# Perceiver block on one core: ten row buffers for the experts, and the turned input weight kept in memory between the batches

## What is computed

```python
x = x + xattn(layernorm(x), ctx)       # softmax(q k^T) v, q from x, k and v from ctx
x = x + ssm(layernorm(x))              # below
x = x + moe(layernorm(x))              # 8 experts, each token goes to the one with the largest gate

def ssm(x):
    xn = layernorm(x)
    xz = xn @ in_w.T + in_b            # in_w: 1024 x 512, two halves: u and z
    u, z = xz[..., :512], silu(xz[..., 512:])
    y = causal_convolution(u)          # length 512, done with sine and cosine tables
    return clip((y * z) @ out_w.T + out_b + x, -10, 10)

def moe(xt):                           # 1024 tokens
    sel = argmax(softmax(xt @ gate_w + gate_b))
    return (xt @ expert_w[sel] + expert_b[sel])
```

## Time and profile before

| | |
|---|---|
| median of 3 runs | 1106.79 us (1106.1 to 1108.63) |
| the profiled execution | 1108.95 us, its span 1107.1 us |
| PE busy | 1070.4 us (97%), weight loads 870.1 us (79%) |
| DVE, ACT, POOL busy | 854.1 us (77%), 537.4 us (49%), 539.5 us (49%) |
| mean granted clock of PE | 0.987 |
| DMA | 182.26 MB, 165 GB/s over the span |
| chain that ended last | PE 81%, DVE 7%, issue 4%, POOL 3%, DMA 2%, SPq 2%, ACT 1% |

### The profile page before, as it was taken

How to read it: one execution, slowest core, us unless ns; L and a number is a source line. 1 busy time by engine, 2 the same in 40 slices (tenths; PEclk the granted TensorE clock), 3 DMA queues, 4 the chain that set the end, 5 groups by cost and what they waited for, 6 DMA issues and landing times.

```text
span 1107.1 us, 16363 instructions
## 1 busy us (share of the span) xinstructions
PE 1070.4 (97%) x4873; PEld 870.1 (79%) x4873; DVE 854.1 (77%) x1786; ACT 537.4 (49%) x1145; POOL 539.5 (49%) x585
## 2 busy tenths in 40 slices
PE   7999999999999999999999999999999999998697
PEld 6887887788888888887778888888888888886585
DVE  7863688898888888888777777777777657799694
ACT  5222165565555555544664444444444443457371
POOL 2544064445444544411276656665766543227365
PEclk9999999999999999999999999999999999999699
DMA  8221577977767777422358877766776552015992
GB/s 299 86 77 38 94 187 192 215 200 199 186 180 189 193 182 186 152 79 90 81 124 202 195 187 197 194 182 182 184 207 172 174 155 77 1 50 192 344 368 92
DMA packets 199398, 182.26 MB, mean 165 GB/s; under 512 B 17920, under 2 KB 144928, under 8 KB 199346
## 3 DMA queue, kind: packets, MB, share of 16 engines
q1 hardware_dynamic: 178706, 140.21, 48.8%
q10 hardware_dynamic: 17280, 31.46, 8.1%
q0 software_dynamic: 3360, 9.97, 2.5%
HBM read 141.73 MB, written 41.68 MB: 166 GB/s over the span
## 4 chain that ended last, share of the span: by engine, by line
PE 81%; DVE 7%; issue 4%; POOL 3%; DMA 2%; SPq 2%; ACT 1%; POOLq 0%; ACTq 0%; DVEq 0%
PE bank L659 41%; PE bank L823 28%; PE bank L668 3%; PE bank L1101 2%; PE bank L676 1%; PE bank L923 1%; DMA vrows<-in_L_attn_log_dt_dram 1%; POOL hl_F L2178 1%; PE bank L1039 1%; DMA resid<-mixed,gather_rows 1%; DMA resid<-p_rows 1%; DVE probs L392 1%; POOL hl_B L2185 1%; POOL spectra L2348 1%; PE bank L876 0%
## 5 line engine op out<-in xcount | busy, mean ns | idle before, releaser
L1251 ACT ACTIVATE probs<-bank,nbias 128x512 f32<-128x512 f32 x128 | 88.2, 689 | 240.1 <-DVE nbias L1750 240.0
L823 PE MATMUL bank<-hl_F,probsT 128*128 128x512 f32 x768 | 190.1, 396 | 1.9 <-issue 1.6
L823 PE MATMUL bank<-hl_A,probsT 128*128 128x512 f32 x768 | 189.9, 396 | 0.0
L659 PE MATMUL bank<-hl_B,hl_D 128*128 128x512 f32 x768 | 186.4, 392 | 2.4 <-POOL hl_B L2185 2.4
L659 PE MATMUL bank<-hl_C,hl_D 128*128 128x512 f32 x768 | 186.2, 391 | 0.0
L1745 DVE TENSOR_REDUCE mx<-bank 128x1 f32<-128x512 f32 x128 | 87.9, 687 | 119.2 <-PE bank L659 119.2
L823 PEld LDWEIGHTS bank<-hl_F,probsT 128*128 128x128 f32 x768 | 144.0, 188 | 36.4 <-issue 1.9
L659 PEld LDWEIGHTS bank<-hl_B,hl_D 128*128 128x128 f32 x768 | 143.8, 188 | 35.1 <-issue 3.3
L823 PEld LDWEIGHTS bank<-hl_A,probsT 128*128 128x128 f32 x768 | 144.0, 188 | 33.9 <-POOL hl_A L2178 0.3
L659 PEld LDWEIGHTS bank<-hl_C,hl_D 128*128 128x128 f32 x768 | 144.2, 188 | 32.4
L2178 POOL TENSOR_TENSOR hl_F<-stage,hl_F 128x512 fp32r<-128x512 f32 x64 | 85.7, 1339 | 163.6 <-ACT hl_F L1216 163.6
(11 more groups left out here) (468 smaller groups left out, 1852.7 us busy)
## 6 DMA issues: line engine op xcount, KB each, us to landing
p_rows<-probs ACTq DMA_DIRECT2D x120, 256.0 KB, 3.3
stage<-in_ctx_dram SPq DMA_DIRECT2D x112, 256.0 KB, 3.1
spectra<-in_ctx_dram SPq DMA_DIRECT2D x64, 256.0 KB, 5.8
xb<-in_ctx_dram SPq DMA_DIRECT2D x64, 256.0 KB, 5.8
resid<-p_rows SPq DMA_DIRECT2D x240, 64.0 KB, 2.0
h<-p_rows SPq DMA_DIRECT2D x120, 64.0 KB, 2.6
obB<-p_rows SPq DMA_DIRECT2D x120, 64.0 KB, 2.0
stage<-in_L_ffn_expert_w_dram SPq DMA_DIRECT2D x6, 1024.0 KB, 5.8
```

What stands on the lines that cost most here:

```text
L659: last = nc.tensor.matmul(dst, lhs[:, a, t, k * P:(k + 1) * P], rhs[:, c, t, :], start=(t == 0 and (a, c) == PASSES[0]), stop=(t == T - 1 ...
L823: last = nc.tensor.matmul(obank[u % 2][:], probsT[u % 2][:, a, j, :], nat[b][par][:, c, j, :], start=(j == 0 and (a, c) == PASSES[0]), sto ...
L1251: nc.scalar.activation(dst, src, ACT.Exp, bias=nbias[:, q:q + 1], scale=SCALE, accum_out=rsum[:, q:q + 1]).then_inc(probs_ready, 1)
```

## The change

The number of row buffers goes from 8 to 10; the two new ones are `probs` and `h`, four arrays of 2 KB that now lie together as `narrow`. The gathers 8 and 9 are issued with the first eight. The jobs `inT0` and `inT1` of batch 1 are gone. In the middle SP stores `hlB` and `hlC` as they are (high and low) to `in_w_kept`, and at the head of its tail POOL loads them back, once the last scores that read them are done. ACT waits for the stores before it overwrites the two, PE for the loads before `u` and `z`. ACT writes the inverse table before, not after, the second half of batch 0's spectrum. SP loads `out_w` earlier.

```diff
-ROWS_KEPT = 8
+ROWS_KEPT = 10
...
-TAIL_JOBS = (tiles_at(1, "inT0", "pooledT", "inT1") + [f"GT.{n}" for n in range(4)] + tiles_at(1, "x_attn")
+TAIL_JOBS = (tiles_at(1, "pooledT") + [f"GT.{n}" for n in range(4)] + tiles_at(1, "x_attn")
...
-AFTER = [JOB[f"inT0.0@{b}"] for b in range(B)]
+AFTER = [JOB["inT0.0@0"], JOB["pooledT.0@1"]]
...
+        narrow = sb("narrow", [P, 4, CH])
+        probs = [narrow[:, n] for n in range(2)]
...
+        h = [narrow[:, 2 + n] for n in range(2)]
...
-        kept = [spectra[:, 2 * n:2 * n + 2, :] for n in range(4)] + [m[:, 2 * n:2 * n + 2, :] for m in (resid0, qc1) for n in range(2)]
+        kept = [spectra[:, 2 * n:2 * n + 2, :] for n in range(4)] + [m[:, 2 * n:2 * n + 2, :] for m in (resid0, qc1, narrow) for n in range(2)]
```

SP, in `load_natural`, in the middle and behind batch 1's attention:

```diff
+                if b == 1 and c >= NCH:
+                    return
...
                 load(f"chunk{c}@1", ctx_rows[NCH + c])
+                sp.wait_ge(evacuated, EVAC[f"inT{c}.3@0"])
+                sp.dma_start(in_w_kept[c], (hlB, hlC)[c][:].bitcast(F32).rearrange("p a t n -> p (a t n)")).then_inc(in_w_put[c], 16)
...
+            sp.wait_ge(nat_split, B * STEPS - T)
+            load("out_w", matrix(out_w))
             sp.wait_ge(p_moved, B * MOVED)
...
-            sp.wait_ge(filled, JOB["inT0.3@1"] + 1)
-            load("out_w", matrix(out_w))
```

PE, in `attention` and `tail`:

```diff
-                pe.wait_ge(in_nat[b][0], 16 * T * (NCH // 2))
...
-                transposes(f"inT0.#@{b}", stage[0])
+                if b == 0:
+                    pe.wait_ge(in_nat[b][0], 16 * T * (NCH // 2))
+                    transposes(f"inT0.#@{b}", stage[0])
                 weigh(TRIPS - 1, UN - 1)
...
+                pe.wait_ge(in_w_back[0], 16)
                 for k in range(T):
                     evacuated_from(f"normT.{k}@1")
                     product(open_bank(f"u.{k}@1")[:], hlA, k, hlB).then_inc(filled, 1)
+                pe.wait_ge(in_w_back[1], 16)
                 z_tiles(range(1))
```

ACT, in `first_chunk`, `attention` and `tail`:

```diff
+                    act.wait_ge(in_w_put[0], 16)
...
+                if b == 1:
+                    act.wait_ge(in_w_put[1], 16)
...
-                round_scaled("inT0.#@1", hlB)
                 round_rows("pooledT.#@1", hlA)
+                act.wait_ge(pv_ready, 2 * STEPS)
+                for n in range(4):
+                    inverse_table(n)
                 for m in range(T):
                     round_output(0, 1, m)
-                round_scaled("inT1.#@1", hlC)
-                for n in range(4):
-                    inverse_table(n)
```

POOL:

```diff
+            def input_weights_back():
+                for c in range(2):
+                    pool.wait_ge(scores_ready, B * STEPS - T * (1 - c))
+                    pool.wait_ge(in_w_put[c], 16)
+                    nc.gpsimd.dma_start((hlB, hlC)[c][:].rearrange("p a t n -> p (a t n)"), in_w_kept[c]).then_inc(in_w_back[c], 16)
             def tail():
+                input_weights_back()
                 outputs_lo()
...
-                for g in range(ROWS_KEPT):
+                for g in range(E):
                     gather(g)
                 pool.wait_ge(indexed, 2)
+                for g in range(E, ROWS_KEPT):
+                    gather(g)
```

More of the change, by code:

```diff
@@ L166, in build @@
         zT = sb("zT", [P, T, S])
-        h = [sb(f"h{n}", [P, S]) for n in range(2)]
+        h = [narrow[:, 2 + n] for n in range(2)]
         resid0 = sb("resid0", [P, T, D])
@@ L300, in build @@
         p_in = [sem(f"p_in{n}") for n in range(2)]
+        in_w_put, in_w_back = ([sem(f"{n}{k}") for k in range(2)] for n in ("in_w_put", "in_w_back"))
         in_nat = [[sem(f"in_nat{b}{n}") for n in range(2)] for b in range(B)]
@@ L308, in build @@
         x_kept = nc.dram_tensor("x_kept", [B, P, T * D], F32)
+        in_w_kept = nc.dram_tensor("in_w_kept", [2, P, 2 * T * D], F32)
         p_rows = nc.dram_tensor("p_rows", [2, P, CH], F32)
@@ L863, in turn_pooled @@
                     turn_rows(f"pooledT.{k}@{b}", rows, k)
-                pe.wait_ge(in_nat[b][1], 16 * T * (NCH // 2))
-                transposes(f"inT1.#@{b}", stage[1])
+                if b == 0:
+                    pe.wait_ge(in_nat[b][1], 16 * T * (NCH // 2))
+                    transposes(f"inT1.#@{b}", stage[1])
             def attend(b, ks):
@@ L1848, in lift @@
                 link(nc.vector.reciprocal(lsum[:], lsum[:]))
-                lo_scaled(f"inT0.#@{b}", hlB)
+                if b == 0:
+                    lo_scaled("inT0.#@0", hlB)
                 lo_rows(f"pooledT.#@{b}", hlA)
-                lo_scaled(f"inT1.#@{b}", hlC)
+                if b == 0:
+                    lo_scaled("inT1.#@0", hlC)
             def attend(b, ks):
```

3 lines of the change are left out of this document (1 added, 2 removed).

## The result

The changed kernel takes **1098.59 us** (median of 8 runs, 1095.34 to 1101.13), the kernel before 1106.28 (8 runs, 1104.28 to 1108.63). The ratio is 0.9925, 95% interval 0.9910 to 0.9941: faster by some 8 us. A second series of the same kernel gave 1099.61 against 1109.38, ratio 0.9921 (0.9899 to 0.9943). A ratio here is not the plain quotient of the two medians, which would be 0.9930 and 0.9912.

The account below looks back on a forecast made before the run. PE, busy for 97% of the span, was taken as the bound. Gains of 5.03 and 4.56 us sum to 9.6, from the median of 1106.79 to 1097.2 us; range 1094.5 to 1102.5.

Parts of the forecast that it names:

- Part 1: End of the second attention: with the turned input weight kept, `x_attn` begins at 916.92 instead of 921.95, gain 5.03 us.
- The shift is carried to the loop: From `x_attn` to the expert loop each step is released by the one before, so the 5.03 us are kept.
- POOL's issues: End of attention: each kept-weight load takes POOL 1 us to issue, upper bound 13; up to 8 each are free.
- The return: Loading 4.2 MB back before `u` and `z.0`: 11 us at 388 GB/s, zero cost; even half that speed still zero.
- The middle at zero: SP's two stores of the kept weight end before ACT overwrites `hlB` at 545.57, so they cost zero.
- Part 2: Expert loop with ten row buffers: gain 4.56 us, 2.67 of it waiting for group 12, the rest slow clock.
- POOL's later gathers move up two places: Expert loop: gathers 12, 13 and 14 take earlier slots, 12 at 1065.78 and 14 at 1079.60; group 12 lands near 1072.6.
- The weights at zero: Expert loop: gathers moved ahead delay weights at most 2.7 us; the tightest, W13, has 3.5 us of cover, so zero.
- a sign of being wrong: Listed signs: ACT waiting for a weight, PE for `in_w_kept`, `outputs_lo` ending after 930, a new wait in the middle.
- Why POOL is slow: Expert loop: POOL's slow DMA instructions (2.69 us against 0.99) seem to wait for DVE's four subtractions.
- the rival of the full queues: Expert loop: full DMA queues slow POOL, gathers or a weight stay late, part 2 lost, 1101.8 us; chance 0.07.
- The profiled execution: Whole kernel: the profiled execution of 1108.95 us becomes 1099.4 us after 9.6 us of gain.

Follow-up runs that it names:

- late_return: Changed kernel with POOL's two loads of the kept weight issued behind its additions of the output bias; 1114.08 us in one run.
- filled_waits: Changed kernel with PE turning the unit matrix, for no one, in five waits of the tail; ratio to the kernel before 0.9908.
- rows_only: Kernel before with ten row buffers instead of eight, its attention as before; 1105.72 us, ratio to the kernel before 0.9964.
- small_loads: Changed kernel with the loads of W8 to W14 cut to one of four row blocks; 1098.54 us in one run.
- small_subs: Changed kernel with VectorE's subtractions for W6 to W14 cut to two of 512 columns; 1095.36 us in one run.

## Why the prediction was right, and where it was off

Forecast 1097.2 us, measured 1098.6, within the range (whose lower end should be 1094.7 by its own sum, 1097.2 less 2.5, not 1094.5). 9.6 us of gain were forecast, about 8.3 measured by the ratio, and 8.8 in the second series (0.79%); the interval of the ratio reaches from 6.5 to 10.0 us, so the sum is not told apart from what came.

- **Part 1**, forecast 5.03 us, is 5.32 to 5.33 in each profile of the changed kernel and of the variants that keep its order. The 0.3 us more are mostly the turned pooled rows, 1.74 us (909.40 to 911.14) where 1.96 were taken. The two things in it that were separated by reasoning (3.3 us of transposes, the rest waits for banks) measured 3.50 and 1.82.
- **The shift is carried to the loop**: right within the noise. From `x_attn` to mix 10, twelve profiles (all but `late_return`) took 157.8 to 160.4 us, the two of the old order 158.9 and 159.2. The clock behind the short waits and a wait for gather 1 of up to 1.2 us (3.3 in `filled_waits`) differ between them. That the first profile kept part 1's gain to within half a microsecond is therefore partly luck.
- **POOL's issues**: taken as 1 us each, measured 0.83 and 0.56. A load of 2.1 MB is issued as fast as a gather of a quarter of that, so the upper bound of 13 us was far off.
- **The return**: 11 us at 388 GB/s were taken; the second landed 15.2 us after the first was issued, 4.2 MB at 275 GB/s beside other traffic, and 13.1 us after it, 319 GB/s, with little else in the queues (`late_return`, 8.2 and 12.3 us to landing). Mis-sized by over a third, with some 30 us of cover. The Trainium skill's figure in "DMA: Bandwidth & Descriptors", section on the anatomy of one DMA, gave an estimated 6.8 us for one; the shortest measured here was 8.2.
- **The middle at zero**: right, even doubled. The second store was issued at 505.56 and landed 11.3 us later, at 516.9; ACT overwrote `hlB` at 543.25.
- **Part 2**, forecast 4.56 us, measured 3.7 in the profile of `rows_only`, 4.6 with both parts (18.04 less the second profile's 13.45), and 0.36% or 4.0 us by the times. The step "POOL's later gathers move up two places" held in six of nine profiles: in the second of the changed kernel gathers 13 and 14 were issued 8.5 and 1.3 us before mix 10 started, as worked out (1072.38 and 1079.60 against 1080.88). In `filled_waits` they came 3.6 us later than that, still without a wait. In the other two it failed: POOL's instructions were held from scatter 2 on, each slot cost 3.6 us from there, the gathers had moved by one pair, and gather 14 was 0.7 us late. The prediction took the slots of one profile as fixed, where their length depends on what VectorE does beside them.
- **The weights at zero**: right for PE, but with nothing to spare. The prediction's cover is a little smaller than it says: 1061.51 and 13.1 make 1074.6, not 1074.3, so 3.3 us. And W13 is not the tightest. In three of the ten-buffer profiles ACT had to wait for a weight, for W14 each time (0.23, 0.91 and 0.52 us) and in two also for others, which was named as a sign of being wrong. PE had no wait from it: ACT's lead over PE took it up. From the second profile of the changed kernel:

```profile
1075.32 2.20 ACT L1451 ACTIVATE hl_D<-zT 128x512 fp32r<-128x512 f32 x4 [0.23 <-DMA zT<-in_L_ffn_expert_w_dram]
```

- **Why POOL is slow**: the reading of one row, that it waits for VectorE, was right, and the rival of the full queues falls with `small_loads`. The Trainium skill, "SBUF — State Buffer", section "Who interferes with whom", infers that such a `tensor_tensor` leaves descriptor generation free; the runs speak against it: 3.3 us beside such a series and 0.99 without (`small_subs`).
- **The profiled execution** was forecast at 1099.4 and took 1096.72. The second last weighing came 3.8 us sooner than in before, which is attention and not the change, and from there on some 1.2 us less was gained than forecast; in the other profiles of kernels with the same attention it came between 3.3 us sooner and 1.1 later.

## What to carry to other kernels

Work that the busiest engine repeats on unchanged data can be bought back with a store and a load, if the load is issued long before its reader: here its price was zero with 25 us in hand and microsecond for microsecond without. When a queue of late instructions is to be brought forward, do not move durations along with slots: an instruction's duration can depend on which of another engine's it falls beside. Before a difference of two profiles is explained, look where it arises: a third of this one (3.8 of 12.2 us) stood ahead of the place that was changed.

## What the runs showed of the hardware

- GpSimd's gathers and scatters took 0.94 to 1.11 us where VectorE's `tensor_tensor` with both inputs in SBUF were cut short, and up to 3.3 beside full series of them (2.49 us for four). The lengthened ones ended 0.9 to 1.0 or 0.3 to 0.4 us before the end of the series, or 0.8 to 0.9 behind it. After one of the last kind, the next one, if it waited for nothing else, fell 0.03 to 0.09 us behind the start of the next series and was held to its end, with one exception, up to VectorE's last series.
- A plain load of 2.1 MB cost GpSimd 0.56 to 0.84 us to issue, and landed 8.2 us later at the soonest.
- A scatter of 128 rows waited for by GpSimd held it 3.3 to 4.5 us before gather 10 (with ten buffers), and 3.7 with the loads of W8 to W14 cut to a quarter.
- Behind one and the same wait of 2.15 us TensorE ran 48 matmuls in 11.18 or in 12.7 to 12.8 us: quick in seven profiles, two of them of the old order, slow in five. With the wait filled by transposes, 11.18 in the one profile taken.
